# A graph layer, linear attention and a two-expert FFN on one core: GpSimd makes every fourth low half, 1.5 row pairs per k step, the lists behind the last pair, the jump ahead of the table's waits, sums from step 17

## What is computed

```python
xn  = layernorm(x)
agg = segment_sum(xn[src], dst, 6250)               # the gather: 100000 rows
gnn = xn @ W1.T + b1 + (agg / deg[:, None]) @ W2.T + b2
q, k, v = relu(xn @ Wq.T), relu(xn @ Wk.T), xn @ Wv.T       # 16 heads of 32
mix = (q @ (k.T v, per head)) / (q @ sum(k)) @ proj.T + proj_b
x   = x + gnn + mix
y   = layernorm(x)
g   = top-2 gates of softmax(attention pooling(y) @ gate_w + gate_b)
out = x + sum over the two chosen experts of g_e * gelu(gelu(y @ w1_e + b1_e) @ w2_e + b2_e)
```

## Time and profile before

| | |
|---|---|
| time, median of 3 runs (lowest to highest) | 1464.06 us (1461.55 to 1466.59) |
| profiled execution | 1465.09 us, its span 1462.9 us |
| mean granted TensorE clock | 0.977 |
| busy | PE 1372.7 (94%), DVE 940.4 (64%), ACT 610.3 (42%), POOL 834.0 (57%) |
| chain that ended last, by engine | PE 50%, POOL 25%, issue 10%, DVE 8%, DMA 4%, ACT 2% |

### The profile page before, as it was taken

One profiled execution on the slowest core, in us unless ns is written; L12 is line 12 of the kernel. 1 busy time (PEld: TensorE's weight loads), 2 busy tenths in 40 slices (PEclk: granted clock), 3 DMA queues, 4 the chain that ended last, 5 costly groups with the idle time before them and its releaser, 6 DMA issues.

```text
span 1462.9 us, 22936 instructions
## 1 busy us (share of the span) xinstructions
PE 1372.7 (94%) x7764; PEld 625.1 (43%) x7764; DVE 940.4 (64%) x2087; ACT 610.3 (42%) x938; POOL 834.0 (57%) x907
## 2 busy tenths in 40 slices
PE   7888989999999999999999999899996889999997
PEld 3444434444444444444444444344442344444443
DVE  8877343222566877777777767666764466776677
ACT  5645223232233444444434444333332436555554
POOL 4653777777777777777777777777777200000000
PEclk9999999999999999999999999999998989999998
DMA  6854889998888888888887777877877341223322
GB/s 202 259 184 166 254 224 245 238 253 236 269 276 262 280 273 272 281 270 280 252 247 237 238 250 236 251 239 234 249 239 239 110 145 49 91 90 115 115 86 100
DMA packets 141205, 312.09 MB, mean 213 GB/s; under 512 B 40050, under 2 KB 42636, under 8 KB 141108
## 3 DMA queue, kind: packets, MB, share of 16 engines
q0 software_dynamic: 62560, 205.05, 46.7%
q1 hardware_dynamic: 62608, 77.26, 16.9%
q10 hardware_dynamic: 15940, 28.54, 5.3%
HBM read 260.53 MB, written 45.52 MB: 209 GB/s over the span
## 4 chain that ended last, share of the span: by engine, by line
PE 50%; POOL 25%; issue 10%; DVE 8%; DMA 4%; ACT 2%; SPq 0%; DVEq 0%; ACTq 0%; POOLq 0%
POOL ring L811 24%; PE bank L857 13%; PE bank L858 12%; PE bank L862 12%; PE bank L928 4%; DMA ring<-table,src_col 2%; PE bank L946 1%; PE bank L947 1%; PE bank L1121 1%; PE bank L996 1%; DVE xT L1669 1%; PE bank L997 1%; PE bank L998 1%; DVE st L1659 1%; DVE ring L2290 1%
## 5 line engine op out<-in xcount | busy, mean ns | idle before, releaser
L811 POOL DMA_INDIRECT ring<-table,src_col x782 | 759.6, 971 | 251.1 <-issue 242.7
L857 PE MATMUL bank<-wts,xT 128*128 128x512 f16 x588 | 226.2, 385 | 3.9 <-DVE wts L1875 2.1
L858 PE MATMUL bank<-wts,xT 128*128 128x512 f16 x588 | 226.0, 384 | 0.0
L928 PE MATMUL bank<-ring,hot 128*32 128x512 f16 x1560 | 121.3, 389 | 40.2 <-DMA ring<-table,src_col 32.1
L857 PE MATMUL bank<-wts,work 128*128 128x512 f16 x392 | 152.5, 389 | 1.5 <-ACT work L1463 1.4
L862 PE MATMUL bank<-wts,xT 128*128 128x512 f16 x588 | 152.9, 383 | 0.0
L858 PE MATMUL bank<-wts,work 128*128 128x512 f16 x392 | 151.6, 387 | 0.0
L1351 ACT ACTIVATE work<-bank,rd 128x512 f32<-128x512 f32 x49 | 33.7, 687 | 187.4 <-DVE rd L1832 186.3
L1899 DVE TENSOR_TENSOR work<-work 128x512 f16<-128x512 f32 x32 | 22.3, 696 | 137.6 <-ACT work L1409 137.4
L862 PE MATMUL bank<-wts,work 128*128 128x512 f16 x392 | 101.1, 380 | 0.0
L1593 ACT ACTIVATE work<-work 128x512 f32<-128x512 f32 x98 | 61.8, 630 | 79.9 <-DVE work L2300 78.8
(11 more groups left out here) (307 smaller groups left out, 2523.8 us busy)
## 6 DMA issues: line engine op xcount, KB each, us to landing
x_rows<-work ACTq DMA_DIRECT2D x51, 256.0 KB
ring<-table,src_col POOLq DMA_INDIRECT x782
work<-in_x ACTq DMA_DIRECT2D x48, 256.0 KB
ring<-x_rows SPq DMA_DIRECT2D x12, 1024.0 KB, 5.1
out_x<-ring SPq DMA_DIRECT2D x12, 1024.0 KB
table<-xT SPq DMA_DIRECT2D x45, 256.0 KB, 3.2
ring<-in_x SPq DMA_DIRECT2D x44, 256.0 KB, 3.3
spilled<-work SPq DMA_DIRECT2D x25, 256.0 KB, 3.8
```

Of the source, the lines that this page charges most:

```text
L811: pool.indirect_dma_start(ring[:, k, :], None, table[:, :], bass.IndirectOffsetOnAxis(ap=ap, axis=0)).then_inc(sem, 16)
L857: mm(out_, wh(c), mh(c), start=first and c == 0, stop=False)
L858: mm(out_, wh(c), ml(c), start=False, stop=False)
L928: r = mm(ps_unit[a:a + WIDE, :], hot[:, u % 2, DEEP * j + k, :], ring[:, slot(n, j), h * D:(h + 1) * D], start=(k == 0 and h == 0), stop=( ...
```

## The change

Seven edits, all in or around the k phase. (1) `pairs_until` goes from 7/5 to 3/2 pairs per step, so that the last pair is handled at step 14 and no longer at step 16, and KP from 16 to 15. (2) GpSimd makes the low half of every tile t with t % 4 == 3 from tile 7 on (11 tiles), right behind its high half, and DVE leaves these out; who waits for low halves now waits for two counters (`lows_done`). (3) From q = 5 on DVE makes the low halves of a pair one pair later (BEHIND). (4) `place_units` and `make_lists` go from steps 13 and 14 to step 15, behind the last pair. (5) GpSimd loads the flag at step 14 and jumps ahead of the waits for the table; the lists are waited for only ahead of the fourth sum step's gathers. (6) The sums start at step 17 instead of 19, with `K_AT` 7.0 instead of 5.0, which moves the whole `PLAN`: at layer 24 it stands at sum step 118 where it stood at 114, and at the end of layer 48 both stand at 191. Tiles 19 and 20 are now turned by DMA, and 31 instead of 25 means go out to DRAM and back. (7) On SP the weights WV and WQ are loaded ahead of the table's last rows instead of behind them, and G1 and G2 later.

```diff
-KP = 16
-FIRST = 19
+KP = 15
+FIRST = 17
+BEHIND = 4
-K_AT, K_STEP, ... = 5.0, 5.75, ...
+K_AT, K_STEP, ... = 7.0, 5.75, ...
+def low_by_pool(t):
+    return t % 4 == 3 and t > 4
+def lows_until(t, by_pool):
+    return sum(low_by_pool(k) == by_pool for k in range(t + 1))
 def pairs_until(i):
-    return min(PAIRS + 1, LEAD + 7 * (i + 2) // 5)
+    return min(PAIRS + 1, LEAD + 3 * (i + 2) // 2)
+        def lows_done(eng, t):
+            after(eng, s["lo_made"], lows_until(t, False))
+            after(eng, s["lo_pool"], lows_until(t, True))
...
 SP, among the table's rows:
+                if r == T - XI + 1:
+                    weight(WV, qkv_w[2 * D:3 * D])
+                if r == T - XI + 3:
+                    weight(WQ, qkv_w[0:D])
                 sp.wait_ge(s["hi_made"], r + 1)
-                sp.wait_ge(s["lo_made"], r + 1)
+                lows_done(sp, r)
...
-            weight(WV, qkv_w[2 * D:3 * D])
-            weight(WQ, qkv_w[0:D])
...
 GpSimd:
                 pool.tensor_copy(natural(t)[:, 0:D - 1], xn32[:, t % XN, 0:D - 1]).then_inc(s["hi_made"], 1)
+                if low_by_pool(t):
+                    pool.wait_ge(s["hi_made"], t + 1)
+                    pool.tensor_tensor(out=natural(t)[:, D:2 * D - 1], in0=xn32[:, t % XN, 0:D - 1],
+                                       in1=natural(t)[:, 0:D - 1], op=ALU.subtract).then_inc(s["lo_pool"], 1)
...
-            pool.wait_ge(s["lists_made"], 1)
-            pool.wait_ge(s["steps_act"], ORDER.index(("src", 1)) + 1)
-            many = slow_tiles(pool)
-            for t in range(T - NS, T):
-                stored(pool, t)
+                if i == LISTS + 2:
+                    pool.wait_ge(s["lists_made"], 1)
+                    pool.wait_ge(s["steps_act"], ORDER.index(("src", 1)) + 1)
+                    many = slow_tiles(pool)
...
+            table_stored()
             for n in range(STEPS_END):
                 u, k = divmod(n, DEEP)
+                if n == RG - 1:
+                    pool.wait_ge(s["lists_made"], 2)
...
 ScalarE, ahead of the normalised rows of tile t:
-                    after(act, s["lo_made"], t - XN + 1)
+                    lows_done(act, t - XN)
...
 VectorE:
+                    if low_by_pool(t):
+                        continue
...
                     rates(q)
                     moments(q)
-                    lows(q)
+                    if q < BEHIND:
+                        lows(q)
+                    if q > BEHIND:
+                        lows(q - 1)
+                    if q == PAIRS:
+                        lows(q)
...
-                if i == LISTS + 1:
+                if i == KP:
                     place_units()
-                if i == LISTS + 2:
                     make_lists()
```

More of the change, by code:

```diff
@@ L619, in turn @@
                 sp.wait_ge(s["hi_made"], t + 1)
-                sp.wait_ge(s["lo_made"], t + 1)
+                lows_done(sp, t)
                 after(sp, s["g_made"], t - OFF + 1)
@@ L643, in _ @@
                     turn(t)
+                if i == FIRST + 2:
+                    sp.wait_ge(s["steps_act"], EDGES_ALL)
+                    weight(G1, gw1)
+                if i == FIRST + 4:
+                    weight(G2, gw2)
                 if i == T - 1:
@@ L800, in _, with table_stored @@
                     firsts()
-            pool.wait_ge(s["lists_made"], 1)
-            pool.wait_ge(s["steps_act"], ORDER.index(("src", 1)) + 1)
-            many = slow_tiles(pool)
-            for t in range(T - NS, T):
-                stored(pool, t)
+                if i == LISTS + 2:
+                    pool.wait_ge(s["lists_made"], 1)
+                    pool.wait_ge(s["steps_act"], ORDER.index(("src", 1)) + 1)
+                    many = slow_tiles(pool)
+            def table_stored():
+                for t in range(T - NS, T):
+                    stored(pool, t)
             def fetch(k, ap, sem):
@@ L983, in turn_tile @@
                 pe.wait_ge(s["hi_made"], t + 1)
-                pe.wait_ge(s["lo_made"], t + 1)
+                lows_done(pe, t)
                 for c in range(2 * C):
@@ L1733, in judge_lists @@
                 link(V.tensor_scalar(slow_i[:], slow[:, 3:4], float(T), None, ALU.mult))
+                dve.sem_inc(s["lists_made"], 1)
             def place_units():
```

17 lines of the change are left out of this document (7 added, 10 removed).

## The result

The changed kernel takes 1471.71 us (median of 7 runs, 1470.78 to 1475.63), the kernel before 1464.97 (7 runs, 1461.55 to 1467.22). The ratio is 1.0059, with a 95% interval of 1.0043 to 1.0076: **slower by 0.6%, where 1444 us and "faster" was forecast.** The profiled execution took 1471.1 us with a span of 1469.2; before it was 1465.1 and 1462.9.

A forecast was written before the change was run, and what follows sets the result against it. The gathers, 1.276 us apart, were taken as the bound, so the end follows the first gather. Moving that from 146.84 to 126 (20.0 us at the table, 0.8 from the jump) gave 1465.1 - 20.8 = 1444.3, stated as 1444; range 1436 to 1456.

The forecast's parts named there:

- The sums: Sum steps 0 to 191: TensorE needs 953 us, gathers leave 975; with 22 us of slack the whole 20.8 reach the end.
- Rival 3: Gathers come early but TensorE can't use it; the ring fills, only layer 48's 11.5 us are won: 1453 us, chance 0.10.
- rival 4: Slower: GpSimd becomes pacemaker of the k steps, 8.4 us each, first gather 12.5 us later: 1477 us, chance 0.05.
- The table: Last table rows issued at 117.7 instead of 138.0, by DVE's work and waits; kept at 118, over a floor of 111.
- 10.4 from eleven low halves on DVE: Ahead of the table: eleven low halves leave DVE, at a mean of 0.95 us each, saving 10.4 us.
- 10 of 13.5 us of waits: Ahead of the table: of DVE's 13.5 us waiting for GpSimd's high halves, 10 go, as low halves come a pair later.
- 3.9 for the lists: Ahead of the table: the lists move behind the last pair, taking 3.9 us off DVE.
- 4 us of contention: GpSimd's 11 new differences cost DVE 4 us ahead of the table, between bounds of nothing and 13.0.
- 6.2 us a step: Pace of the k steps, 6.85 us before, with step 14's k32 at 111 to 112.
- The jump: GpSimd's branch, 6.25 us of issue before the first gather, moves behind step 15's split; 0.8 us more gained under cover.
- The tail: The stretch behind the last gather stays 315 to 320 us.
- TensorE at the first sum step: TensorE stands there by about 130 and waits some 5 us for gathers, at no cost while gathers are the bound.

The follow-up runs named there:

- e5: The kernel before the change, with only its table of sum steps planned with `K_AT` 1.0 instead of 5.0: 1486.21 us, ratio 1.0152 to before.
- e6: e1 with DVE making all low halves, GpSimd none: 1452.64 us, ratio 0.9900 to the kernel before.
- e1: The changed kernel with its table of sum steps planned with `K_AT` 4.0 instead of 7.0: 1452.87 us, ratio 0.9931 to the kernel before.
- e9: e7 with DVE making all low halves, GpSimd none: 1446.83 us, ratio 0.9895 to the kernel before.
- e7: e2 with the table of sum steps planned with `K_AT` 2.0: 1453.50 us, ratio 0.9921 to the kernel before.
- e10: e3 with DVE making all low halves, GpSimd none: 1450.72 us, ratio 0.9908 to the kernel before.
- e3: The changed kernel with sums from step 19 and `K_AT` 5.0, so the `PLAN` of before: 1450.94 us, ratio 0.9913 to the kernel before.
- e11: e4 with DVE's low halves made a pair later from pair 5 on: 1452.14 us, ratio 0.9924 to the kernel before.
- e4: The kernel before with only GpSimd's early jump, ahead of the waits for the table: 1459.47 us, ratio 0.9965 to before.
- e8: e1 with DVE making a pair's low halves in the pair's own step again: 1465.15 us, ratio 0.9986 to the kernel before.
- e12: e10 with 1.4 pairs a step and `KP` 16: 1448.36 us, ratio 0.9906 to the kernel before.
- e2: The changed kernel with DVE making the low half of units ending in part 1 ahead of `normal`: 1450.61 us, ratio 0.9901 to the kernel before.

## Why the prediction was wrong, point by point

**The bound was read rightly.** "The end is the first gather plus a constant, as long as TensorE keeps up" holds in eleven of the twelve kernels tried: first to last gather 999.7 to 1005.8 us, and 313 to 319 behind it. The changed kernel and e5 are the two in which TensorE did not keep up.

**The step that failed** is in *The sums*: that `PLAN` having TensorE four steps further on "only holds it back until they land", and that 22 us of slack over the whole keep the gathers the bound. The slack of 975 against 953 us is a sum over 191 steps, and TensorE cannot use it where it likes: it can't run ahead of gathers that have not landed, so it can only be as late as the ring is deep. Three waits of 4.2, 4.6 and 4.2 us within 47 us, and a lower clock behind each, went past that. TensorE's waits for DVE in the old trace (8.1 us, none above 1.3) stood in my 953 as they were, although they are a property of the table, and the table was new. The order of both engines showed it before the run: in it `unit_low` of part 1 stands behind `weigh`, and step 75 in part 2.

**Rival 3 had the mechanism** (the ring fills, GpSimd waits for the sum step, a new `PLAN` places sums badly, and the 22 us speak against it), with a chance of 0.10. Its price was the error: I let it keep the 11.5 us of layer 48 as a gain and gave it no loss. It measured a loss of 20.4 against a gain of 13.7. It was the rival with the other sign, and I had given that place to rival 4, GpSimd as pacemaker at 7.9 us a step; the steps took 6.94.

**The table, forecast at 117.7 (118 with the floor), came at 129.46.** Of these 11.5 us 9.9 stand at step 14's k32 (121.39, forecast 111.5) and 1.6 between it and the last rows. Term by term:
- *10.4 from eleven low halves on DVE.* DVE's busy time for low halves fell from 39.2 to 29.2, as said. It bought nothing that shows: with all of them back on DVE the first gather came 3.0 us earlier (e6 against e1), 2.3 earlier (e9 against e7) and 0.8 later (e10 against e3), all within the scatter.
- *10 of 13.5 us of waits.* They vanished at L1701 and came back as 16.2 at L1678. In e11, where nothing else was moved, 8.5 of 13.5 came back. Net the lag is worth 6.1 us (e11 against e4), or 11.9 beside GpSimd's low halves (e8 against e1).
- *3.9 for the lists.* `place_units` and `make_lists` went behind, but `judge_lists` did not: with its reduction of 128x261 and what follows, it holds DVE for 3.4 us on the chain of the changed kernel, whose first and last such pieces are:

```profile
114.74 1.25 DVE ring L1758
...
117.97 0.17 DVE slow_i L1765
```

  The moved lists and weights together measured 3.6 (e12 against e11), which is the size forecast but no more than the scatter of single profiles, so this term is neither shown nor refuted.
- *4 us of contention.* GpSimd's high halves gained 115 ns each over 43, its differences 112 over 16: 6.7 us on GpSimd, where I had looked only at DVE's side. Most of it comes with the lag and not with GpSimd's new work (814 ns in e11). The base was misread too: the two low halves of 1.59 us that the prediction calls alone had the first of them (0.99) beside GpSimd's second cast, and alone a low half takes 0.68, so the mean of 0.95 held such meetings already. What the lag changed is which engine comes second. The Trainium skill (SBUF — State Buffer, SBUF: two separate sides) has whichever starts first hold the shared port for the whole instruction and the other one block. The trace agrees on who loses (e11 above), but the cast lost 0.45 us there while the low half still had 0.59 to run.
- *6.2 us a step* was the sum of these; it was 6.94.

**The jump** was right: 6.25 us became 0.88, and alone it gave 5.8 us of first gather and 0.35% of the time (e4). I had booked only 0.8 for it, because the table was to be ready before step 15's split; with the table 12 us later than forecast, the table is the cover and the jump gives nearly its whole length. The sum itself slipped by 1: 1444.3 less the 1.0 is 1443.3, and 1444 was given.

**The tail** of 315 to 320 us was right, 315.5.

**TensorE at the first sum step** was to wait about 5 us and waited 4.83; that it costs nothing is not refuted. But in the k phase (130 to 372) it waited 15.1 us for gathers against 8.5, and the last k32 came at 371.38 against 367.23, so being placed further on did hold TensorE back there. e2 has 16.4 us of that same wait and a median of 1450.61: by itself it is paid from the slack.

## What to carry to other kernels

A change that makes the bound stream start earlier often brings a new plan for the rest, and the new plan has to be read as a change of its own: for each place where a consumer's step follows the last step of a unit, look at what stands ahead of the unit's closing work on the other engine. A slack that was summed over a long stretch did not cover a cluster of three stalls, while a single longer one cost nothing; compare stalls with the buffer between the two engines, at their place, and count the lower clock behind them. And when a wait is removed by making its work later, ask for which engine the same instruction will wait next: here 8.5 of 13.5 us came back one line further up.

## What the runs showed of the hardware that was not expected

GpSimd's cast of 128x511 took 602 to 623 ns, or 968 to 1081 where it began while a low half ran on DVE, and a low half took 681 ns alone and 1112 on average where it began while an instruction of GpSimd was running (the kernel before and e11): of two instructions that met, the later was the longer one. TensorE's waits of 4.2 to 4.6 us each ended with matmuls of some 0.6 us in place of 0.38, at a granted clock of 0.50 to 0.60 in the 3 us behind. Not each long wait did so: after one of 3.14 us in the changed kernel (at 407.11) the clock was 0.50, after one of 3.52 in e1 (at 977.58) 1.00. With the stalls 21 us apart, a stretch of 70 us then had a granted clock of 0.90 and 115 of 425 matmuls less, 18.9 us of work for 13.0 us of waits. The mean of 782 gathers differed between kernels from 968 to 977 ns with the same code, 7 us over all of them, and for this I have no cause.
